# Five written-out instruction orders in place of one shared step schedule, in a macaron block (FFN, attention, FFN) over 16 batches

## The reference, cut to what matters

```python
x = x + 0.5 * ffn(layernorm(x))          # x: 16 batches x 512 rows x 256, float32
x = x + attention(layernorm(x))          # 16 heads of 16, rope on q and k, softmax
x = x + 0.5 * ffn(layernorm(x))

def ffn(x):
    base = x @ W_base + b_base
    h = relu(x @ W_enc[n] + b_enc[n])                     # for 8 adapters n
    recon = h @ W_dec[n] + b_dec[n]
    top1 = argmin_n mean((recon - x) ** 2)                # one adapter per batch
    adp = connected_idx[top1]
    mid = relu(x @ W_down[adp] + b_down[adp])
    return base + mid @ W_up[adp] + b_up[adp]
```

## Time and profile before

| | |
|---|---|
| median of 3 runs | 2008.59 us (2006.72 to 2010.13) |
| the profiled execution | 2006.77 us |
| its span from first to last instruction | 2005.0 us |
| PE, DVE, ACT, POOL busy | 1821.8, 1312.2, 979.7, 494.8 us |
| mean granted TensorE clock | 0.969 of full |

### The profile page before, as it was taken

One profiled execution on the slowest core, in us unless ns is written; L12 is line 12 of the kernel. 1 busy time (PEld: TensorE's weight loads), 2 busy tenths in 40 slices (PEclk: granted clock), 3 DMA queues, 4 the chain that ended last, 5 costly groups with the idle time before them and its releaser, 6 DMA issues.

```text
span 2005.0 us, 26466 instructions
## 1 busy us (share of the span) xinstructions
PE 1821.8 (91%) x9128; PEld 998.4 (50%) x9128; DVE 1312.2 (65%) x2795; ACT 979.7 (49%) x1954; POOL 494.8 (25%) x665
## 2 busy tenths in 40 slices
PE   6499999899999999999999999999999998999876
PEld 4344455455455544555455454555545454554434
DVE  5567675767767576766757677675767767676531
ACT  1236464645536464553645555364545536455531
POOL 1404040412304041230504123050321405032101
PEclk8698999999999999999999999999999999999997
DMA  4423232212333221333331233333123333204100
GB/s 108 74 43 64 43 64 43 51 33 45 64 54 64 43 45 33 50 64 53 64 43 39 36 54 64 53 56 51 35 41 53 64 54 56 41 27 69 22 11 11
DMA packets 96715, 99.38 MB, mean 50 GB/s; under 512 B 19972, under 2 KB 88261, under 8 KB 96453
## 3 DMA queue, kind: packets, MB, share of 16 engines
q1 hardware_dynamic: 93830, 97.16, 28.0%
q10 hardware_dynamic: 2752, 0.54, 0.2%
HBM read 63.54 MB, written 33.55 MB: 48 GB/s over the span
## 4 chain that ended last, share of the span: by engine, by line
PE 64%; DVE 17%; ACT 8%; issue 6%; POOL 4%; DMA 0%; ACTq 0%; POOLq 0%; SPq 0%; DVEq 0%
PE ps L559 9%; PE ps L622 9%; PE ps L606 9%; PE ps L535 7%; PE ps L547 6%; PE ps L664 5%; DVE mx L872 5%; PE ps L624 5%; DVE xn L903 3%; ACT pr L762 3%; PE ps L727 3%; PE ps L665 3%; PE ps L646 2%; ACT xn L787 2%; PE ps L711 1%
## 5 line engine op out<-in xcount | busy, mean ns | idle before, releaser
L762 ACT ACTIVATE pr<-ps 128x512 f32<-128x512 f32 x1024 | 555.9, 598 | 464.4 <-PE ps L547 462.4
L872 DVE TENSOR_REDUCE mx<-ps 128x1 f32<-128x512 f32 x1024 | 654.4, 682 | 155.9 <-PE ps L535 152.7
L547 PE MATMUL ps<-stack 98*128 98x512 bf16 x1024 | 325.7, 387 | 32.6 <-ACT pr L762 24.7
L535 PE MATMUL ps<-stack 96*128 96x512 bf16 x1024 | 322.0, 384 | 28.3 <-DVE mx L872 27.0
L559 PE MATMUL ps<-pr,va 128*32 128x512 f32 x2048 | 275.1, 609 | 0.0
L922 DVE SCALAR_TENSOR_TENSOR ps<-ps,wb,h 128x512 f32<-128x512 f32 x128 | 96.8, 756 | 190.2 <-PE ps L624 190.2
L547 PEld LDWEIGHTS ps<-stack 98*128 98x128 bf16 x1024 | 86.6, 100 | 210.6 <-issue 95.3
L535 PEld LDWEIGHTS ps<-stack 96*128 96x128 bf16 x1024 | 100.0, 98 | 180.0 <-DVE mx L872 80.3
L812 ACT ACTIVATE h<-ps,benc 128x512 f32<-128x512 f32 x128 | 88.1, 688 | 199.8 <-PE ps L606 199.8
L1132 POOL CAST wdh<-wd_all 128x128 fp32r x32 | 9.5, 296 | 653.9 <-DVE adapter L950 586.6
L606 PE MATMUL ps<-xh,w_eh 128*128 128x512 f32 x256 | 118.5, 463 | 34.9 <-ACT wu_mT L779 26.2
(11 more groups left out here) (151 smaller groups left out, 3036.7 us busy)
## 6 DMA issues: line engine op xcount, KB each, us to landing
stack<-scratch SPq DMA_DIRECT2D x384, 128.0 KB, 6.2
scratch<-parts SPq DMA_DIRECT2D x64, 384.0 KB, 2.3
xin<-in_L_attn_x_dram SPq DMA_DIRECT2D x16, 512.0 KB, 3.9
out_dram<-x SPq DMA_DIRECT2D x16, 512.0 KB, 6.7
stack<-wu_mT SPq DMA_DIRECT2D x128, 4.0 KB, 1.7
cst<-in_const_dram SPq DMA_DIRECT2D x1, 1024.0 KB
raw<-in_L_ffn_W_dec_dram ACTq DMA_DIRECT2D x1, 512.0 KB, 5.6
pr<-in_L_ffn_W_enc_dram SPq DMA_DIRECT2D x2, 256.0 KB, 7.7
```

The source lines that it names most:

```text
L535: pe.matmul(bank1[:, t % 2, :], stack[0][0:KB, hd, 128 * t:128 * t + 128], stack[1][0:KB, hd, :], start=True, stop=True).then_inc(s1_full. ...
L547: pe.matmul(bank2[:, a % 2, :], stack[1][:, 4 * g + a, 128 * t:128 * t + 128], stack[0][:, 4 * g + a, :], start=True, stop=True).then_inc( ...
L762: act.activation(pr[:, n % 2, a, :], bank2[:, a % 2, :], ACT.Exp, scale=SCALE).then_inc(ex_done.sem, 1)
L872: dve.tensor_reduce(mx[:, hd // 4 % 2, e:e + 1], bank1[:, t % 2, :], AX.X, ALU.max).then_inc(mx_done.sem, 1)
```

## The change

1. `schedule` is replaced by five functions, one for each engine (`tensor_order`, `scalar_order`, `vector_order`, `gpsimd_order`, `sync_order`), each with the period's steps written out. The steps are the same 127 (PE), 71 (ACT), 82 (DVE), 18 (POOL) and 14 (SP) that do something, in another order. `walk` starts one number earlier and passes over what `enter` has done.
2. `normalise` on DVE (L903) becomes a `scalar_tensor_tensor` whose second factor is `rs` broadcast over 256, in place of a `tensor_scalar` with two per-row scalars.
3. `cost` makes 32 equal rows and not 128: `ones` is 128x32, and `loss`, `tiny`, `adapter` and the chain of `pick` are on 32 partitions.
4. The one-time weight preparations `w1` and `w2` are called from the first `gr` and the first `pick`; they stand at the same place of DVE's sequence.

The moves, by engine. Batches are written as in `stage(name, ahead, ...)`, ahead of or behind the period's own; lines with - are the old place, with + the new.

```diff
# PE
   op -1 0 | s2 0 3 0 | s1 0 8 0 | mt 0 1 | op -1 1
+  pv 0 2
   s2 0 3 1
+  tr +1 2 0
   s1 0 8 1
-  pv 0 2
-  tr +1 2 0
   tr +1 2 1
   s2 0 4 0
+  pv 0 3
   s1 0 9 0 | s2 0 4 1
+  qk +1 0
   s1 0 9 1
-  pv 0 3
...
   qk +1 2 | s2 0 7 0 | s1 0 12 0 | mt 0 2
+  pv 0 6
   en -1 1 1 | qk +1 3 | s2 0 7 1 | s1 0 12 1
-  pv 0 6
...
# DVE
   op -1 0
+  lx +1 2 0
+  lx +1 2 1
   s1 0 8 0 | op -1 1 | st -1 1 0
+  st -1 1 1
-  lx +1 2 0
-  lx +1 2 1
   s1 0 8 1
-  st -1 1 1
-  s1 0 9 0
   tl +1 2 0 | tl +1 2 1
+  s1 0 9 0
...
   va +1 1
+  ro3 +1 0
   ms 0 2
-  ro3 +1 0
...
   ro1 +1 3 | lx +2 0 0
-  lx +2 0 1
   s1 0 13 1 | gr -1 1 0
+  lx +2 0 1
   s1 0 14 0 | gr -1 1 1
...
+  s1 0 4 0
   cost +1 0 | pick +1 0
-  s1 0 4 0
   s1 0 4 1
...
   up +1 0 1 | st +1 2 0
+  st +1 2 1
   s1 0 7 0
-  st +1 2 1
...
-  pick -1 1                 (last of the period)
+  pick -2 1                 (after s1 0 0 1 of the next period)
# ACT
-  s2 0 7 0 | mt 0 2 | en -1 1 1 | ro3 +1 1
+  mt 0 2 | ro3 +1 1 | s2 0 7 0 | en -1 1 1
# POOL
-  zs +1 0 (first), ... ro2 +1 1 | zs -1 1 | ro1 +1 2 ... b0 +1 | pick -1 1
+  ... ro1 +1 3 | zs -1 1 | ro2 +1 3 | b0 +1 | pick -1 1 | zs +2 0 (last)
# SP
-  mt -1 3 (first)           + mt 0 3 (last)
   mt 0 0 | lift 0 2 | lift 0 3
+  load +2
   store -2
-  load +2
   mt 0 1
+  mt 0 2
   ro3 +1 0
-  mt 0 2
...
```

```diff
-  dve.tensor_scalar(xn[s][:, t, 0:D], src[:, t, :], mv[s][:, t, 0:1], rs[s][:, t, :],
-                    ALU.subtract, ALU.mult)
+  dve.scalar_tensor_tensor(out=xn[s][:, t, 0:D], in0=src[:, t, :], scalar=mv[s][:, t, 0:1],
+                           in1=rs[s][:, t, :].to_broadcast([128, D]), op0=ALU.subtract, op1=ALU.mult)
-  pe.matmul(bank[:, 0:N], ones, zt[f][:, 0, :], start=True, stop=False)
-  pe.matmul(bank[:, 0:N], ones, z[f][:], start=False, stop=True)
+  pe.matmul(bank[0:32, 0:N], ones, zt[f][:, 0, :], start=True, stop=False)
+  pe.matmul(bank[0:32, 0:N], ones, z[f][:], start=False, stop=True)
```

More of the change, by code:

```diff
@@ L101 @@
 LAG = 5
[L104 to L262, removed]
@@ new lines, in gpsimd_order, with sync_order @@
+def gpsimd_order(stage):
+    stage("pick", +1, 0)
+    stage("rs", +1, 2)
+    stage("rs", -1, 1)
+    stage("ro1", +1, 0)
+    stage("tl", -1, 1, 0)
+    stage("tl", -1, 1, 1)
+    stage("ro2", +1, 0)
+    stage("ro1", +1, 1)
+    stage("ro2", +1, 1)
+    stage("ro1", +1, 2)
+    stage("rs", +2, 0)
+    stage("ro2", +1, 2)
+    stage("ro1", +1, 3)
+    stage("zs", -1, 1)
+    stage("ro2", +1, 3)
+    stage("b0", +1)
+    stage("pick", -1, 1)
+    stage("zs", +2, 0)
+def sync_order(stage):
+    stage("mt", 0, 0)
+    stage("lift", 0, 2)
+    stage("lift", 0, 3)
+    stage("load", +2)
+    stage("store", -2)
+    stage("mt", 0, 1)
+    stage("mt", 0, 2)
+    stage("ro3", +1, 0)
+    stage("ro3", +1, 1)
+    stage("lift", +1, 0)
+    stage("lift", +1, 1)
+    stage("ro3", +1, 2)
+    stage("ro3", +1, 3)
+    stage("mt", 0, 3)
@@ L265, in enter, with walk, stage @@
+BEGIN = (("load",), ("st", 0, 0), ("st", 0, 1), ("rs", 0), ("lx", 0, 0), ("lx", 0, 1), ("tr", 0, 0), ("tr", 0, 1))
 def enter(do):
     first = Batch(0)
-    for name, args in (("load", ()), ("st", (0, 0)), ("st", (0, 1)), ("rs", (0,)), ("lx", (0, 0)), ("lx", (0, 1)),
-                       ("tr", (0, 0)), ("tr", (0, 1))):
+    for name, *args in BEGIN:
         if name in do:
             do[name](first, *args)
-def walk(do):
-    for number in range(-1, B + 2):
-        schedule(do, number)
+def walk(order, do):
+    for number in range(-2, B + 2):
+        def stage(name, ahead, *args):
+            b = Batch(number + ahead)
+            if 0 <= b.number < B and not (initial(b) and (name, *args) in BEGIN):
+                do[name](b, *args)
+        order(stage)
@@ L521, in lift @@
                                  scratch[b.odd][k][:, :, part, :].rearrange("h d n -> d h n")).then_inc(stacked[k].sem, 16)
-            walk(dict(load=load, store=store, mt=maxima, ro3=put, lift=lift))
+            walk(sync_order, dict(load=load, store=store, mt=maxima, ro3=put, lift=lift))
             sp.wait_ge(*stored.at(Batch(B - 1), 0))
@@ new lines, in dense_weights @@
+            def dense_weights():
+                link(dve.tensor_copy(w_bh[:], w_b))
+                dve.tensor_tensor(w_bl[:], w_b, w_bh[:].bitcast(F32), ALU.subtract).then_inc(s_split, 1)
+                for raw_w, w in ((q_raw, w_q), (k_raw, w_k), (v_raw, w_v)):
+                    link(dve.tensor_copy(w[0][:], raw_w))
+                    last = dve.tensor_tensor(w[1][:], raw_w, w[0][:].bitcast(F32), ALU.subtract)
+                    if w is not w_v:
+                        link(last)
+                last.then_inc(s_split, 1)
@@ L1033, in dense_weights @@
-            def dense_weights():
-                link(dve.tensor_copy(w_bh[:], w_b))
-                dve.tensor_tensor(w_bl[:], w_b, w_bh[:].bitcast(F32), ALU.subtract).then_inc(s_split, 1)
[L1037 to L1041, removed]
-                last.then_inc(s_split, 1)
```

372 lines of the change are left out of this document (330 added, 42 removed).

## The result

| | before | after |
|---|---|---|
| median of the runs | 2008.45 us (2006.72 to 2010.13, 4 runs) | 1844.35 us (1842.72 to 1845.85, 4 runs) |
| span of the profiled execution | 2005.0 us | 1840.9 us |
| one period (13 whole ones) | 117.1 to 118.3 us, mean 117.65 | 106.5 us in ten; 106.9, 107.0 and 108.4 in the others; mean 106.74 |
| granted TensorE clock over the span | 0.969 | 0.976 |

It comes from the periods: 10.9 us in the mean of the 13 whole ones (141.8 us), and 22.3 us in all that lies before and behind them, which is what the two partial periods at the ends would give (2 x 10.9). So lead-in and tail did not matter, as said; a period gained 10.9 us and not 4.4.

A forecast was written before the change was run, and what follows sets the result against it. PE's work plus its idle time was taken as the bound, only idle time winnable. Terms 1.65 + 1.4 + 0.45 + 1.3 + 0.1 gave 4.9 us, less 0.5: 4.4 x 15 periods = 66 us, so 1941 us, range 1912 to 1985.

The forecast's parts named there:

- the low end: Fastest time of the range: all 6.0 us of PE idle time and 0.45 of clock gone in 15 periods, 1910 us.
- The move at `op`: L903 directly behind half 0 of `op`: waits before transposes and `s2` go, 2.3 less 0.65 new, net 1.65 us per period.
- The third `mt`: ACT's copy ahead of exponentials, `pv` before `en`: 1.78 us gap goes, 0.35 back for `ms` behind rope, net 1.4 per period.
- The clock: Clock falls only behind the third `mt` gap, so 0.9 us of every other period goes: 0.45 per period, between 0 and 0.45.
- The maxima: PE's waits for DVE around 872, 917 and 940 us: 1.3 of 1.6 us per period gone, bounds 0.3 and 1.6.
- The form of L903: New DVE instruction in `normalise` expected near 425 ns against 410: 0 us per period, bounds -0.1 and +0.5.
- The store behind the load: On SP, `load` ahead of `store`; store expected to land before DVE L1003 needs its buffer: 0, bounds 0 and 2.2 us per period.
- the rival: Store lands late, DVE stands 0.6 to 1.9 us at L1003 and PE at the second `mt`: 1950 to 1970 us, chance 0.14.
- POOL and SP at nothing: New orders of POOL and SP have microseconds to spare at each user, the store aside: 0 us per period.
- The reserve of 0.5: 0.5 us per period kept back from the 4.9 us sum for waits that a walk through the orders overlooks.
- the waits only move: Idle time set by a loop through ACT, POOL and DVE reappears at next `s2` or `s1`: 2000 to 2010 us, chance 0.10.
- the second rival: Second in the prediction's list: DVE's longer blocks hold the maxima, 2.8 us per period back, 1983 us; with other new waits 0.17.

The follow-up runs named there:

- e13: e1 with exponentials and row maxima taken over 256 of 512 columns, all matmuls kept: 1945.13 us, ratio 0.9691.
- e9: The changed kernel with `cost` on 128 columns again: 1845.63 us, ratio 0.9186.
- e10: The changed kernel with five `pv` of a period put back directly behind their `s1`, ahead of the dense piece: 1859.67 us, ratio 0.9259.
- e2: e1 with PE's `pv` 6 moved between the third `mt` and `en`, and ACT's copy of that `mt` ahead of two exponentials: 2003.62 us.
- e1: The changed kernel with all five engine orders put back to the old ones, new L903 form and `cost` on 32 columns kept: 2019.09 us, ratio 1.0052.
- e6: The changed kernel with POOL's and SP's orders put back to the old ones; PE, DVE and ACT new: 1843.74 us, ratio 0.9176.
- e12: The changed kernel with the old form of L903 and DVE's `ms` of the third group ahead of `ro3` 0 again: 1834.85 us, ratio 0.9134.

## Why the prediction was wrong

**The step that failed** is the first: "So the time is PE's work plus PE's idle time, and a new order can only win the idle time." Busy time was taken for work. Its window of 110.6 us held about 3.9 us of waits (10.5 by distances, 6.6 marked) and 2.1 us that depend on neighbours and on `cost`, which gives 110.6 - 6.0 = 104.6; the change reached 106.0 (0.7 of waits inside the busy time and 0.6 of small excesses are left or new). With it fell the low end, "all 6.0 us of idle time and 0.45 of clock gone". Of the 4.6 us by which busy time fell, e13 shows 1.1 by shorter waits alone, and e9 the 0.26 of `cost`. e10 supports the part of succession: five places put back raise PE's busy time by 0.69 us. The split of the rest, over half of the 4.6, is by distances and was not isolated by a run.

The Trainium skill warns of this measure, in Trainium Kernel Development and Optimization, section "Performance Expectations": matmul busy time is a bad metric for closeness to the roofline, because matmuls are pipelined, and the use of the peak rate (MFU) and the busy share of the weight loads are the good ones. The trace agrees: the loads are busy 60.68 us in a period before and 60.59 after, so their share rose from 52 to 57%, while matmul busy time went from 110.6 to 106.0.

**The move at `op`** (forecast 1.65): right in mechanism. L903 stands directly behind half 0 of `op`, and `tr` follows `pv` and `s2` with no wait. DVE, then ACT of after:

```profile
874.74 0.69 DVE L1224 TENSOR_TENSOR x<-ps,x 128x512 f32<-128x512 f32 x1 [0.27 <-PE ps L905]
875.34 1.66 DVE L1119 SCALAR_TENSOR_TENSOR xn<-x,mv,rs 128x256 f32<-128x256 f32 x4
```

```profile
883.06 2.08 ACT L965 ACTIVATE xn<-x,shift,rs 128x256 f32<-128x256 f32 x4 [0.45 <-POOL shift L1258]
```

ACT's wait for `shift` is 0.45 and not 1.68. Of 2.29 marked, 0.29 came back. Under-sized: the two `s2` pairs after it also lost 0.28 each inside their busy time.

**The third `mt`** (forecast 1.4, bounds 0 and 1.3 for what comes back): 1.85 by distance, 0.24 back. But e2 shows that it is not a term by itself: alone it wins 1.0 per period.

**The clock** (forecast 0.45): the size is right (117.65 in the mean beside 117.2 for a period at 1.00), since every whole period of after has 1.00. The periods did not quite alternate, six of 13 had the fallen clock. The reason holds at most in part: in e2 the gap was gone and the clock fell in four periods (eight in e1); in e13 a gap of 1.34 us stayed there, and it fell in one.

**The maxima** (forecast 1.3, bound 1.6): all 1.6 gone, and more by distance (`s1` to `gr` 1.48, `s1` to `en` 0.31, `s1` to `s2` 0.51, less 0.31 that after still has at `s1` to `en`: 2.0), plus most of 0.92 before `pv`. The bound of 1.6 was again a sum of marks.

**The form of L903** (forecast 0, 425 ns): it takes 477 ns, and costs about 4 us in the new orders and, with `cost`, 10 in the old. By the Trainium skill, VectorE: DVE Perf Modes, section "The perf-mode tier table", a float32 `tensor_scalar` within SBUF runs at twice the rate of an instruction with two tensors. The trace does not agree: the old form takes 410 ns beside 425 for the `tensor_tensor` and 477 for the new form, so the swap cost 67 ns each, and not the 0.1 us that the prediction worked out from that rule.

**The store behind the load** (forecast 0, bounds 0 and 2.2): right for most periods, but the rival did occur in some. SP's queue in after, in two periods:

```profile
654.06 0.40 SPq L646 DMA_DIRECT2D xin<-in_L_attn_x_dram  x1
654.50 0.51 SPq L678 DMA_DIRECT2D out_dram<-x  x1
...
868.81 0.40 SPq L646 DMA_DIRECT2D xin<-in_L_attn_x_dram  x1
869.25 1.28 SPq L678 DMA_DIRECT2D out_dram<-x  x1
```

The later of these stores landed 4.9 us after its start, at 874.2, 0.6 us ahead of L1224; its issue of 1.28 us is the only one of that length, the other eleven behind a load took 0.51. The earlier one landed after 7.1 us, at 661.64. DVE stood until then, and PE at the second `mt` behind it, as the rival said:

```profile
661.66 0.69 DVE L1224 TENSOR_TENSOR x<-ps,x 128x512 f32<-128x512 f32 x1 [1.95 <-DMA out_dram<-x]
...
662.41 0.23 PE L756 MATMUL ps<-ident_b,mx 128*32 128x128 bf16 x1 [1.70 <-DVE x L1224]
```

Over the whole run this is what the group of L1224 waited for:

```profile
L1224 DVE TENSOR_TENSOR x<-ps,x 128x512 f32<-128x512 f32 x32 | 22.0, 686 | 12.0 <-PE ps L905 8.7 <-DMA out_dram<-x 3.2
```

3.2 us of DMA in four places. Two of them reached PE in whole periods, with 0.51 and 1.70 us: they are after's periods of 107.0 and 108.4 us, some 2.3 us in all and not 9 to 29. The prediction named a wait of L1003 for the landing as a sign that it is wrong; the sign came, in a few periods. e6, with the old SP and POOL orders, has no such wait in its whole periods and the same time as after (its plain period is 106.60 us and not 106.54), so the two cancel.

**POOL and SP at nothing**: right (e6). **"The reserve of 0.5" and "the waits only move"**: the runs show why the second rival was not foolish. With one or two engines' orders waits do move or grow. They go when PE, DVE and ACT change together, and then the gain is more than the sum of the steps: +68, +8 and +29 alone, -175 together.

**What stays open.** Which of the 1.8 us of succession is the bank, the shape or the weight load; what `cost` on 32 columns is worth (0 to 4 us); whether store before load with all else as after would save the 2.3 us (e12 has the same waits, 1.15 us the longest); and what makes the clock fall in some periods of the old orders and in none of the new.

## What to carry to other kernels

When an in-order engine is the bound, do not take its busy time for its floor: compare the distance from start to start of the same pair of stages at all its places, and count what exceeds the smallest as waiting. Move long work of the bound engine between a request to another engine and its use, and change the orders of the engines that answer at the same time, since one order alone can look harmful (+68 us) that is needed for the gain (-175 us). Look at the granted clock of every period before you put such a loss down to waits. And time each form of an instruction before swapping it: the swap in this change went the wrong way by 67 ns each.
